# A gated cross-attention block with routed experts on one core: the query rows' layernorm factor turned on TensorE instead of sent through DRAM

## What is computed

```
q = lora_proj(layernorm(x)) ; k, v = lora_proj(ctx)        # 16 heads of 16
p = softmax(q*SCALE @ k.T + attn_bias)                     # bias: (128, 16, 128, 128)
x = x + tanh(g_xattn) * (p @ v)
xf = layernorm(x); e = argmax(softmax(xf @ Wg + bg))       # one of 8 experts per token
x = x + tanh(g_ffn) * (gelu(xf @ W1[e] + b1[e]) @ W2[e] + b2[e])
```

## Time and profile before

| | |
|---|---|
| median of 3 runs | 2023.44 us (2020.26 to 2023.89) |
| the profiled execution's own time | 2008.24 us |
| its span, first to last instruction | 2006.4 us |
| PE / DVE / POOL / ACT busy | 1373.5 / 1137.6 / 1000.9 / 774.8 us (68% / 57% / 50% / 39%) |
| DMA traffic | 288.73 MB, mean 144 GB/s |
| granted TensorE clock, mean | 0.835 of full speed |

### The profile page before, as it was taken

One profiled execution on the slowest core, in us unless ns is written; L12 is line 12 of the kernel. 1 busy time (PEld: TensorE's weight loads), 2 busy tenths in 40 slices (PEclk: granted clock), 3 DMA queues, 4 the chain that ended last, 5 costly groups with the idle time before them and its releaser, 6 DMA issues.

```text
span 2006.4 us, 41833 instructions
## 1 busy us (share of the span) xinstructions
PE 1373.5 (68%) x12568; PEld 1150.0 (57%) x12568; DVE 1137.6 (57%) x2377; ACT 774.8 (39%) x1660; POOL 1000.9 (50%) x1051
## 2 busy tenths in 40 slices
PE   4656666666666566666666656666666666999998
PEld 3545555555555455555555545555555555788887
DVE  3445555565655555556555555555555555855655
ACT  1333334444434334444443334444333344533333
POOL 2334544555554455455554544555445454655455
PEclk7777878888877778888887888888777788999999
DMA  4555655555555555556555555556555554599896
GB/s 114 125 120 126 132 129 119 115 130 130 131 131 114 122 129 128 102 129 131 131 128 110 128 128 123 110 126 131 121 114 131 129 129 113 198 297 278 277 284 212
DMA packets 156729, 288.73 MB, mean 144 GB/s; under 512 B 36836, under 2 KB 72166, under 8 KB 156544
## 3 DMA queue, kind: packets, MB, share of 16 engines
q1 hardware_dynamic: 142992, 252.02, 54.7%
q0 software_dynamic: 12624, 34.62, 4.7%
q10 hardware_dynamic: 1056, 1.39, 0.2%
HBM read 251.89 MB, written 36.98 MB: 144 GB/s over the span
## 4 chain that ended last, share of the span: by engine, by line
DMA 71%; PE 14%; SPq 9%; issue 5%; POOL 0%; DVE 0%; ACT 0%; POOLq 0%; ACTq 0%
DMA rs_dram<-x2n 70%; PE two L789 5%; PE bank L803 5%; SPq L403 5%; SPq L367 2%; PE two L777 1%; DMA RS<-rs_dram 1%; SPq L357 0%; PE two L596 0%; PE bank L630 0%; PE bank L621 0%; DMA w_sb<-in_w 0%; PE two L646 0%; SPq L398 0%; DMA rows_dram<-vacant 0%
## 5 line engine op out<-in xcount | busy, mean ns | idle before, releaser
L596 PE MATMUL two<-KT,QT 32*128 32x256 f32 x2048 | 206.1, 532 | 599.6 <-DVE QT L1104 564.0
L485 POOL TENSOR_TENSOR sc<-sc,negmax 128x1024 f32<-128x1024 f32 x256 | 484.1, 1893 | 149.9 <-DVE negmax L1045 144.3
L596 PEld LDWEIGHTS two<-KT,QT 32*128 32x128 f32 x2048 | 125.1, 250 | 636.6 <-DVE QT L1104 493.4
L1039 DVE TENSOR_TENSOR sc<-two,sc 128x1024 f32<-128x1024 f32 x256 | 312.1, 1219 | 130.2 <-PE two L596 128.8
L507 POOL TENSOR_SCALAR ve<-mv 128x2 f32<-128x2 f32 (+1 forms) x135 | 30.5, 226 | 667.8 <-DVE mv L1068 654.9
L1045 DVE TENSOR_REDUCE negmax<-sc 128x8 f32<-128x1024 f32 x256 | 312.4, 1220 | 16.2
L621 PE MATMUL bank<-cst,sc 128*128 128x128 f32 x2032 | 287.6, 287 | 0.1
L887 ACT ACTIVATE PT<-bank 128x512 f32<-128x512 f32 x508 | 279.5, 603 | 15.6 <-PE bank L621 14.4
L853 ACT ACTIVATE QT<-QT,cst 128x256 f32<-128x256 f32 x128 | 58.0, 500 | 559.4 <-DVE QT L1104 559.4
L621 PEld LDWEIGHTS bank<-cst,sc 128*128 128x128 f32 x2032 | 239.1, 148 | 32.7 <-issue 32.2
L1055 DVE BATCH_NORM_STATS2 st<-x_sb 128x6 f32<-128x256 f32 x128 | 53.9, 421 | 358.0 <-DMA x_sb<-in_x 356.1
(11 more groups left out here) (159 smaller groups left out, 2059.0 us busy)
## 6 DMA issues: line engine op xcount, KB each, us to landing
sc<-in_bias SPq DMA_DIRECT2D x256, 512.0 KB
w_sb<-in_w SPq DMA_DIRECT2D x69, 257.0 KB, 3.7
CT<-in_w SPq DMA_DIRECT2D x69, 256.0 KB, 3.8
xg<-rows_dram SPq DMA_DIRECT2D x63, 272.0 KB, 3.8
x_sb<-in_x SPq DMA_DIRECT2D x128, 128.0 KB, 11.0
CT<-in_ctx_in SPq DMA_DIRECT2D x64, 256.0 KB
XT<-in_x_turned SPq DMA_DIRECT2D x64, 256.0 KB
RS<-rs_dram SPq DMA_DIRECT2D x128, 64.0 KB
```

The lines of the kernel that those rows point to most:

```text
L485: nc.gpsimd.tensor_tensor(s, s, m, ALU.add).then_inc(sub_ok, 1)
L596: ins = mm(b_s[j][:, 2 * P * c:2 * P * c + 2 * P], QT[rows, pair, c, P * sq:P * sq + P], KT[rows, pair, c, sq].rearrange("p e k -> p (e k) ...
L1039: nc.vector.tensor_tensor(s, two[h][:], s, ALU.add).then_inc(s_used, 2)
```

## The change

The DRAM tensor, its write and its read are gone, with their semaphores. In the even step that projects the queries of a pair, TensorE now does two transposes, one per sequence of the pair, ahead of the query projection: the operand is the factor's column broadcast along the free axis to 128x128, so that the turned result holds the row on every partition. They write columns 256 to 511 of `b_x`, the same PSUM bank as the value projection. ScalarE copies the 128x256 block into `RS`, which has one buffer now. The value projection of even steps waits for this copy (`rs_evac`), and so does VectorE's `scale_queries`.

```diff
-            def send_scale(t):
-                sp.wait_ge(rs_ok, t.n(1, 1))
-                sp.nop(nofuse=True)
-                sp.dma_start(rs_dram[t.n()], ln[:, (t.k - 7) % 8, 0, 0:1]).then_inc(rs_out, 16)
-
-            def spread_scale(t):
-                pair = t.k // 2 % 2
-                if t.reached(4):
-                    sp.wait_ge(scaled_ok, t.per(2, 1, -1))
-                    sp.nop(nofuse=True)
-                sp.wait_ge(rs_out, t.n(16, 16))
-                sp.nop(nofuse=True)
-                tok = P * t.slot(2)
-                sp.dma_start(RS[:, pair, tok:tok + P], rs_rows[t.n()].partition_broadcast(P)).then_inc(rs_in[pair], 16)
...
+                if qry and qry.slot(2) == 0:
+                    pe.wait_ge(rs_ok, qry.n(1, 2))
+                    if not cur and val.reached(1):
+                        pe.wait_ge(v_evac, val.n())
+                    for n in range(2):
+                        rs = ln[:, (qry.k + n - 7) % 8, 0, 0:1].broadcast_to([P, P])
+                        ins = nc.tensor.transpose(b_rs[:, P * n:P * n + P], rs, ident)
+                    ins.then_inc(rs_ready, 1)
...
-                    if not cur and val.reached(1):
+                    if qry and qry.slot(2) == 0:
+                        pe.wait_ge(rs_evac, qry.per(2, 1, 1))
+                    elif not cur and val.reached(1):
                         pe.wait_ge(v_evac, val.n())
...
+                if qry and qry.slot(2) == 0:
+                    act.wait_ge(rs_ready, qry.per(2, 1, 1))
+                    nc.scalar.copy(RS[:], b_rs).then_inc(rs_evac, 1)
...
-                dve.wait_ge(rs_in[pair], t.per(4, 32, 32))
+                dve.wait_ge(rs_evac, t.per(2, 1, 1))
```

More of the change, by code:

```diff
@@ L105, in sem @@
             return ctx.enter_context(nc.semaphore(name))
-        rs_dram = nc.dram_tensor("rs_dram", (N, P, 1), F32, kind="Internal").ap()
-        rs_rows = rs_dram.rearrange("n p a -> n a p")
         rows_dram = nc.dram_tensor("rows_dram", (DUMMY + FT, ROW), F32, kind="Internal").ap()
@@ L135, in flamingo_block @@
         sc = sb("sc", [P, 4, HEADS * P])
-        RS = sb("RS", [P, 2, 2 * P])
+        RS = sb("RS", [P, 2 * P])
         XT = sb("XT", [P, 2, KC, 2 * P])
@@ L202, in flamingo_block @@
         b_x, b_o = bank[6], bank[7]
-        b_v, b_x2 = b_x[:, 0:HID], b_s[3]
+        b_v, b_rs, b_x2 = b_x[:, 0:HID], b_x[:, HID:HID + 2 * P], b_s[3]
         o_ps = b_o[:].rearrange("p (h c) -> p h c", c=CELL)
@@ L254, in flamingo_block @@
         xT_in = [sem(f"xT_in{i}") for i in range(2)]
-        rs_out, rs_in = sem("rs_out"), [sem(f"rs_in{i}") for i in range(2)]
+        rs_ready, rs_evac = sem("rs_ready"), sem("rs_evac")
         s_setc, scaled_ok = sem("s_setc"), sem("scaled_ok")
@@ L352, in _ @@
             load(cst[:, 0:C_FIRST], consts[:, 0:C_FIRST], s_id)
-            def send_scale(t):
-                sp.wait_ge(rs_ok, t.n(1, 1))
-                sp.nop(nofuse=True)
-                sp.dma_start(rs_dram[t.n()], ln[:, (t.k - 7) % 8, 0, 0:1]).then_inc(rs_out, 16)
-            def spread_scale(t):
-                pair = t.k // 2 % 2
-                if t.reached(4):
-                    sp.wait_ge(scaled_ok, t.per(2, 1, -1))
-                    sp.nop(nofuse=True)
-                sp.wait_ge(rs_out, t.n(16, 16))
-                sp.nop(nofuse=True)
-                tok = P * t.slot(2)
-                sp.dma_start(RS[:, pair, tok:tok + P], rs_rows[t.n()].partition_broadcast(P)).then_inc(rs_in[pair], 16)
             def step(i, k):
                 behind = seq(i, k, -4)
-                if behind and not (isinstance(i, int) and k < 0):
-                    send_scale(behind)
                 t = seq(i, k, -6) if k > FIRST else None
@@ L390, in step @@
                     sp.dma_start(XT[:, behind.k // 2 % 2], x_turned[behind.per(2)]).then_inc(xT_in[behind.k // 2 % 2], 16)
[L391 to L394, removed]
                 t = seq(i, k, -3)
@@ L1100, in scale_queries @@
                 pair = t.k // 2 % 2
-                dve.wait_ge(rs_in[pair], t.per(4, 32, 32))
+                dve.wait_ge(rs_evac, t.per(2, 1, 1))
                 for o in range(KC):
                     dve.wait_ge(q_ready, t.per(2, KC, o + 1))
-                    ins = nc.vector.tensor_tensor(QT[:, pair, o, :], b_s[o][:, 0:2 * P], RS[:, pair, :], ALU.mult)
+                    ins = nc.vector.tensor_tensor(QT[:, pair, o, :], b_s[o][:, 0:2 * P], RS[:], ALU.mult)
                 ins.then_inc(scaled_ok, 1)
```

## The result

| | before | changed kernel |
|---|---|---|
| median | 2023.05 us (4 runs, 2020.26 to 2023.89) | 1337.1 us (4 runs, 1333.63 to 1339.41) |
| ratio | | 0.6609, 95% interval 0.6593 to 0.6626 |
| the profiled execution's own time / span | 2008.24 / 2006.4 us | 1339.41 / 1337.6 us |
| one step of the first stage | 13.25 us | 8.00 us |
| first scores' bias addition | 38.1 us | 23.4 us |

The change made the kernel a third faster.

The account below looks back on a forecast made before the run. The landing of SyncE's column write to DRAM was taken as the bound. 2008.24 less 603 (127 periods, 13.25 to 8.5) less 10 at the start gave 1395, by ratio 1406; forecast 1405 us, range 1345 to 1520.

Parts of the forecast that it names:

- Most of the time belongs to the write itself: First stage, column write to rs_dram: 11.1 us of landing a step, 8.3 us at the start with no bias issued.
- The third rival: x_sb waits for the queue, not the write; landing stays 11.0 us, 13.05 a step, 1973 us; chance 0.04.
- Removed wait: First stage: 128 writes, 128 reads and SyncE's wait go; SyncE had stood 1166.8 us over 126 waits.
- landing of x_sb: First-stage load of x_sb: landing near 4 us expected, for a median of 11.0 before.
- clock: PE's clock in the first stage: above 0.95 expected, for a mean of 0.81; scores at 1.15 us.
- one RS buffer: RS with one buffer: the next copy comes a pair later, behind L1104 anyway; costs nothing.
- Additions at nothing: Two transposes on PE and a 128x256 copy on ACT per pair: taken as 0, bounds 0 and 44 us.
- Scatter hidden: GpSimd's scatter to rows_dram: 2.3 us plus landing of 2.8 makes 5.1 a step, taken as hidden.
- rival 1: First stage: scatter's landing takes the write's place; period 9.2 gives 1484 us, typically 10 or 1585; chance 0.18.
- The period: First-stage step: 13.25 us falls to 8.5, bounds 7.9 and 9.2; over 127 periods a gain of 603 us.
- jitter: First-stage step: 0.1 us added where two nearly equal engines hand over.
- Start: DVE's first L1104 waits 9.97 us for RS: 10 us saved, bounds 0 and 14.

Follow-up runs that it names:

- the wide write: Kernel before, column write made one of 64 KB (128 rows of 512 bytes, from the identity), spread read of its first row: 1346.57 us, ratio 0.6898.
- the doubled and the missing ones: Changed kernel with added transposes and copies twice per pair (1324.67 us), or for the first pair only (1325.66 us); unchanged on that chip 1323.96 us.

## Why the prediction was right and where it was wrong

- **"Most of the time belongs to the write itself": right for its elements side by side, and stronger than I had it.** I took the loss for a chain of waits through SyncE. The write alone, with nobody waiting for its landing, keeps the period at 11.89 us; the chain without the neighbouring small elements has 8.07 to 8.14. The third rival (the queue) is out by the wide write, which has the same queue ahead of it. That x_sb lands early without these writes was more than the earlier trace rows could tell, since all its loads stand in the first stage; the changed kernel shows it.
- **Removed wait, landing of x_sb, clock, one RS buffer: right.** x_sb lands after 2.1 us (I said near 4), the clock is 1.00 (above 0.95), scores take 1.15 us.
- **Additions at nothing: right**, by the doubled and the missing ones. The cover was the even step's DVE work, as the forecast had it.
- **Scatter hidden: right** for the changed kernel. GpSimd's wait for it is 1.9 us in all there, 78.5 with the wide write, and 574.3 with the column write alone. So the mechanism that rival 1 feared is real, and it is the column write that drives it, not what the change leaves behind.
- **The period, 8.5 for 8.00: the step that failed.** An odd step was forecast at 7.83 and takes 7.81 on average (7.3 without, 8.3 with the gate's product). The even one was forecast at 8.48 and takes 8.26 from one L1029 to the next. There I took 1.43 us from the scores to L1039, read in an odd step; in the even step, from 605.58 to 606.82, it is 1.24. To their average I added 0.25 for the expert choice and 0.1 for jitter. That was wrong. The expert choice runs on DVE from 597.28 to 598.51, while PE, held up by L669's work in the same odd step (L646 in the changed kernel), brings the scores from 597.05 on. L1029 starts 1.47 us behind the scores, for the 1.24 of the even step: of 1.23 us of expert choice 0.23 shows. The two delays lie side by side and I summed them. The run with five more operations shows that this cover is used up: there the step grew by 1.5 us for 1.53. The trace shows nothing that takes the place of the jitter. So 0.25 + 0.1 + 0.12 of the average of 8.5 are accounted for, to 8.03 in the middle of the stage; 0.03 comes from its two ends.
- **The range.** The bound that I had worked out, 7.9 a step or 1315 us for a profiled execution, holds the result. I cut it to 1345 because it needs a period without any hand-over lost, and no row showed such a loss; the period even came out below the 8.16 that the two steps of the sum average to without one.
- **From the profile to the median: wrong.** I raised 1395 to 1406 by the ratio of before, 0.8%. The changed kernel's median is 2.3 us under its profiled time. The kernel before varies more from chip to chip (1948 to 2023 us) than the changed one (1324 to 1337).
- **Start:** 14.7 us for the 10 forecast, just outside the bound of 14. **End:** 12.4 us that nothing in the profile of before could tell, and that are absent on another chip. They are luck for the forecast: without them it would have missed by 80 us instead of 68.

In sum: the periods saved 63.5 us more than forecast and the start 4.7; the ratio put on the forecast is 10, and the median lies 2.3 below the profiled time; the end takes 12.4 back. Together they make the 68 between 1405 and 1337.

The Trainium skill's page "DMA: Bandwidth & Descriptors" was weighed in the forecast. Its fixed 2.0 us (Anatomy of one DMA), given for transfers that GpSimd issues, is near x_sb in the changed kernel, 2.1 us, and far from the 11.0 and 6.6 of the two runs with neighbouring 4-byte elements for which the profile gives this landing. The same page says that under 512 bytes SDMA reads, modifies and writes (Specifications). By that alone, the 4-byte elements 64 bytes apart and the 64-byte ones would be slow too; at periods of 8.11 and 8.08 us this kernel shows little of it. What it says of a semaphore that waits for earlier writes on any queue (Queues, rings and completion order) agrees with the scatters, on GpSimd's queue, that land late in the run with the write alone; no run here tells this cause from another.

## What to carry to other kernels

When the chain that ended last is one tiny transfer, find out whether the wait for it or the transfer itself is the cost, by keeping it and taking away the wait: here the write alone, with nobody waiting for it, cost 3.9 us a step. In this kernel a column of one number per partition must not be written side by side into DRAM every step; 64 bytes between the elements (0.11 us a step left, read included), or a transpose on TensorE, are nearly free. When delays of a step are summed, note first on which engine and beside what each of them runs, and do not narrow a worked-out bound for a loss that no row shows.

## What the runs showed of the hardware that was not expected

- 128 elements of 4 bytes, side by side in DRAM, once per step: period 11.89 us against 8.00 without, with no engine waiting for them before four steps later. 64 or 512 bytes apart: 8.11 and 8.07 in kernels that also wait for them.
- With such a write in every step, the DMA engines are busier and move less (a share of 0.80 and 129 GB/s, for 0.62 and 197 in the changed kernel), and the scatters of another queue land late: after 10.8 us in the median of the run with the write alone.
- A read of one 512-byte row into 128 partitions, 64 KB a step, next to 1.5 MB of other transfers, had no price (8.02 us a step).
- At the border of the stages VectorE and ScalarE stood idle for some 8 us (7.82 and 8.25) in some runs, with nothing in the profile that releases them; the end is 295.4 us there, and 282.2 on another chip.
